# Four residual graph layers in one kernel: a new instruction order between layers 0 and 1 and between layers 2 and 3

## The chip, the cores and the metric

One core of a Trainium2 chip runs the whole kernel in one launch. The metric is the device time of the launch in microseconds (us). Kernels are compared by the median of several runs. The profile is one execution, and its own time stands beside the median below.

## What is computed

Input `x` is 16 batches of 512 nodes x 128 features (f32), `adj` a sparse 512 x 512 matrix. Four layers follow each other, each as `x = layernorm(x + layer(x))`:

```python
# layer 0: eight Euler steps of a graph diffusion
h = einsum('bnd,ed->bne', x, fc_in_w) + fc_in_b
repeat 8: h = h + dt * (alph * 0.5 * (adj @ h - h) + h @ w_eff - h + x0)
# layer 1: normalized graph convolution with two batch norms (statistics over all batches)
agg = einsum('nm,bmd->bnd', A_hat, x);  h = relu(batchnorm(agg @ W1.T + b1));  out = batchnorm(h @ W2.T + b2)
# layer 2: masked attention, 4 heads of 32
scores = q @ k.T / sqrt(32) + mask(adj);  out = softmax(scores) @ v
# layer 3: graph attention with leaky relu scores
e = leaky(s1[:, None] + s2[None, :]) masked by adj;  out = softmax(e) @ (x @ W)
```

## The kernel before

Every engine (PE = TensorE, ACT = ScalarE, DVE = VectorE, POOL = GpSimd, SP = the DMA issuer) has one program of its own, executed in order. Engines meet only in semaphores: `wait_ge` holds an engine's queue until another engine has counted far enough. The order of each engine's work is written out by hand as strings of short item names, and the text below calls an item by its name and batch, as E4.15 for the exponential number 4 of batch 15.

**Layer 0** (`layer0`, from L186) works in 8 groups of two batches. The steps run in a software pipeline `pairs(engine, groups, 5, step)`: step s works on group s (items y, g), on group s-1 (z, p, n, a) and on group s-2 (N, A). `ORDER` (L310) is the order in the middle of the loop, `LAST` (L327) that of step 8, `LATE` (L332) that of step 9. On DVE, p takes a product out of PSUM into `zf` (L684), z forms the low half of a split number (L675), n and N are the layer norm's statistics for the two halves of a group (`statistics` L137 with L141, `aggregate` L143 with L147), and a and A apply the norm and write `X` (`apply`, L182). Between them POOL forms the inverse root (`root`, L149, lines L154 and L156). PE's item p (L893, in `three_pass`, L59 to L61) waits for the low halves z, and its accumulations for the p that freed its bank. `pairs` unrolls the first steps, runs a hardware loop over the middle and unrolls the last ones.

**Layer 1's first half** begins inside steps 8 and 9 of layer 0, since the last products of layer 0 leave gaps. For each batch b: ACT copies the batch to a rounded high part (`batch_high`, L423, line L427); POOL subtracts it for the low part (`batch_low`, L554, line L556, two buffers); PE aggregates (`aggregate`, item a on L963); ACT takes the high part out (L432) and DVE the low part (`aggregate_low`, L648, line L650); PE multiplies by W1 (`hidden`, L973), which waits for that low part; ACT takes it out into `Hb` (L438); DVE adds bn_stats over `Hb` (L817), whose results nobody needs before the end of the layer. PE runs a(b+1) ahead of hidden(b). On POOL, step 9 runs batch_low 2 and 3, then both roots of group 7, and behind the loop come batch_low 4 and 5, two memsets (L595), then batch_low 6. On DVE, step 9 is `#a2 N A`; behind the loop, `aggregate_step` (L809) runs bn_stats for batches 0 and 1, then aggregate_low 3, and so on.

**Layers 2 and 3** (`layers2_3`, L1513) run a loop over 16 batches with about eight steps in flight, and then a hand-written `tail` in which the last batches of layer 2 are mixed with the first of layer 3 (items that begin with 3). Of layer 2, per batch: t0 to t3 on PE are the transposed scores of one head each (L1930, L1934), E0 to E7 on ACT their exponentials, two per head (L1753); S0 to S3 on POOL add the two halves of each head's probabilities (L1678, needs E1, E3, E5, E7 in turn, and the denominators D of the batch before); D0, D1 on PE are the denominators (L1942, wait for all four S); V0 to V3 on PE are the values (L1952, wait for all eight E); e on ACT takes the denominators out (L1763), f the values (L1767); d, o on PE turn both (L1963, L1958); c1, c2 on DVE divide (L1828, L1835; c2 waits for y of the batch before); r on POOL adds the residual (L1684, waits for c2); b on DVE and g2 on POOL are the norm's statistics and root; y on ACT applies it (L175). Of layer 3: 3x turns a batch on PE (L1450), 3XR and 3X on ACT take it out, 3j and 3i on PE form the score rows (L1469, L1476), 3q on PE builds the masked scores (L1499, L1500), 3e on DVE sums, 3E on ACT is the exponential (L1341), 3a on PE the product (L1488).

The tails end, for the last batches:

```python
# POOL
tail("g2.13 S0.15 S1.15 S2.15 r.14 S3.15 g2.14", ...)
# ACT
"... 3W0.0 E2.15 E3.15 f.14 3W1.0 E4.15 E5.15 e.14 E6.15 E7.15 3G.0 3L0.0 3L1.0 y.13 3XR.1 ..."
# PE
"... V2.14 V3.14 3w1.0 t2.15 D0.14 D1.14 3i.0 t3.15 d.14 o.14 V0.15 V1.15 3x.1 V2.15 V3.15 3j.1 D0.15 D1.15 3q0.0 ..."
```

Of the kernel before, what the change touches and what calls it, by code (L numbers as in the profile page):

```python
# [24 lines left out]
ACT = mybir.ActivationFunctionType  # L25
# [56 lines left out]

def pairs(eng, steps, depth, step, first=0, last=None):


    def alive(s):
        return [0 <= s - k < steps for k in range(depth)]

    lead = (depth - 1) + (depth - 1) % 2
    lead = max(lead, first - first % 2)  # L90
    for s in range(first, lead):
        step(s, s % 2, alive(s), s // 2)
    with eng.Fori(lead // 2, steps // 2) as r:
        for parity in range(2):
            step(r * 2 + parity, parity, [True] * depth, r)
    for s in range(steps, steps + depth - 1 if last is None else last + 1):
        step(s, s % 2, alive(s), s // 2)
# [88 lines left out]
def layer0(nc, m, ins, bank, L1):  # L186
# [3 lines left out]
    with ExitStack() as own:  # L190
# [109 lines left out]

        STAGE = dict(h=0, y=0, g=0, z=1, p=1, n=1, a=1, N=2, A=2)

        def order(text):
            items = []
            for word in text.split():
                what, k = (word[:2], int(word[2:])) if word[0] in "#" else (word, sum(w == word for w, _ in items))
                items.append((what, k))
            return items
# [20 lines left out]
            "ACT": order("#x0 #x1 z z z z #a0 z z z z #a1 #h0 #x2 #x3"),  # L329
            "DVE": order("N z z z z A p p #a0 p #w0 p z z z z p p p p #a1 n #W0 #v0 a"),  # L330
        }
        LATE = {"PE": ORDER, "ACT": ORDER, "DVE": order("#a2 N A")}  # L332

        def order_of(s, engine):
            if not isinstance(s, int):
                return ORDER
            return {0: FIRST[engine], 1: SECOND[engine], 2: THIRD[engine], groups: LAST[engine], groups + 1: LATE[engine]}.get(s, ORDER)

# [195 lines left out]
        def _(pool):  # L534
# [30 lines left out]
            def step(s, par, alive, nth):  # L565
# [13 lines left out]
                if alive[2]:  # L579
                    for u in range(2):  # L580
                        norm.root(pool, (s - 2 + CREDIT) * 2 + u, u)
                if isinstance(s, int) and s == 1:
# [4 lines left out]
            pairs(pool, groups, 5, step)  # L587
            for b in range(4, 6):
                batch_low(b, b - 4)
            pool.wait_ge(la_x_lo, after(5, 1))  # L590
# [16 lines left out]
        def _(dve):  # L607
# [46 lines left out]
            def step(s, par, alive, nth):  # L654
                for what, k in order_of(s, "DVE"):
# [21 lines left out]
                    elif what == "p":  # L677
# [8 lines left out]
                    elif what in "nN":  # L686
                        u = "nN".index(what)
                        b = s - STAGE[what]
# [117 lines left out]

            pairs(dve, groups, 5, step)

            def aggregate_step(s, par, alive, nth):  # L809
                early = isinstance(s, int) and s < 4  # L810
                if alive[1] and not early:
                    aggregate_low(s - 1, 1 - par)
                if alive[2]:
                    b = s - 2
                    for c in range(CH):
                        dve.wait_ge(la_h_sb, after(b, CH, c + 1))
                        dve.bn_stats(L1.st1[:, c, bass.ds(b, 1)].rearrange("p a n -> p (a n)"),  # L817
                                     Hb[:, bass.ds(b, 1), c].rearrange("p a n -> p (a n)")).then_inc(la_h_st, 1)

            pairs(dve, B, 5, aggregate_step)  # L820

# [319 lines left out]
def layer3(nc, own, m, bank, out, rl1_at, ready):  # L1141
# [296 lines left out]
    def pe_items(pe):  # L1438

        def item(name, b, par, nth):  # L1440
            what, k = name[0], int(name[1]) if name[-1].isdigit() else 0
            if what == "x":
# [3 lines left out]
                if is_batch(b, 1):  # L1446
                    pe.wait_ge(*ready["second wide"])
                pe.wait_ge(wh_c, after(b - 1, 2))
# [64 lines left out]
def layers2_3(nc, m, bank, wide, out, L1):  # L1513
# [4 lines left out]
    with ExitStack() as own:  # L1518
# [3 lines left out]
        def sem(name):  # L1522
# [16 lines left out]
                 for h in range(2)] + late,  # L1539
# [29 lines left out]
                       {"O": (bn, after(B - 1, 1)), "X": norm.s_x, "score banks": (s_mx, after(B - 1, TILES)),  # L1569
                        "second wide": (t_exp, after(B - 1, EXPS)),  # L1570
                        "ring": ((rcp, after(B - 1, 1)), (o_n, after(B - 1, 1)))})
# [78 lines left out]
        def _(pool):  # L1650
# [39 lines left out]
            third.pool_copy(pool, 1, 1, first=True)  # L1690
            tail("g2.13 S0.15 S1.15 S2.15 r.14 S3.15 g2.14", POOL_ORDER, work, None)
            third.pool_copy(pool, 2, 0, first=True)
# [6 lines left out]
        def _(act):  # L1699
# [13 lines left out]
            def work(name, b, bp, s, alive):  # L1713
# [50 lines left out]
                elif name == "f":  # L1764
# [6 lines left out]
            tail("E0.14 E1.14 E2.14 E3.14 f.13 vc.15 E4.14 E5.14 e.13 nr.15 E6.14 E7.14 3XR.0 3X.0 y.12 E0.15 E1.15 3W0.0 "  # L1771
                 "E2.15 E3.15 f.14 3W1.0 E4.15 E5.15 e.14 E6.15 E7.15 3G.0 3L0.0 3L1.0 y.13 3XR.1 3L2.0 3L3.0 3X.1 f.15 e.15 "
                 "3E0.0 3W0.1 3W1.1 y.14 3E1.0 3XR.2 3G.1 3L0.1 3L1.1 3X.2 3L2.1 y.15", ACT_ORDER, work, item)
# [77 lines left out]
        def _(pe):  # L1851
# [25 lines left out]
            def product(name, b, bp, s, alive):  # L1877
# [82 lines left out]
                elif name == "d":  # L1960
# [7 lines left out]
            pe.wait_ge(third.const, 3)  # L1968
            tail("v.15 t2.14 D0.13 D1.13 n.15 t3.14 3x.0 d.13 o.13 t0.15 3j.0 V0.14 V1.14 t1.15 3w0.0 V2.14 V3.14 3w1.0 t2.15 "
                 "D0.14 D1.14 3i.0 t3.15 d.14 o.14 V0.15 V1.15 3x.1 V2.15 V3.15 3j.1 D0.15 D1.15 3q0.0 3q1.0 d.15 3w0.1 3q2.0 "  # L1970
                 "3w1.1 3q3.0 o.15 3i.1 3x.2 3a0.0 3j.2 3a1.0 3q0.1 3q1.1 3a2.0", PE_ORDER, work, item)
# [38 lines left out]
```

## Time and profile before

| what | us |
|---|---|
| median of 3 runs | 944.48 (944.11 to 945.14) |
| the profiled execution, its own time | 941.33 |
| its span, first to last instruction | 939.5 |
| PE busy | 865.5 (92%) |
| DVE busy | 625.7 (67%) |
| ACT busy | 506.1 (54%) |
| POOL busy | 404.5 (43%) |
| mean granted clock of TensorE | 0.987 of full speed |

A row of the timeline gives start, duration, engine, line, operation, output<-input, shape and count; in square brackets stands how long the engine was idle before, and what released it. Rows of the same kind that follow each other are merged (x4), and the duration is then from the first start to the last end. PE's matmuls overlap, so the next one can start before the one before it has ended. A row of the windows gives the stretch, then each engine's busy time with its count of instructions, the granted clock, the share of DMA and its GB/s.

### The profile page before, as it was taken

How to read it: one execution, taken by the hardware profiler on the slowest of the kernel's cores; microseconds unless marked ns; L12 is line 12 of the kernel's file. 1: busy time of each engine (PE TensorE's matmuls, PEld its weight loads, DVE VectorE, ACT ScalarE, POOL GpSimd, SP SyncE). 2: the span in 40 equal slices, each digit the busy share in tenths (PEclk: the TensorE clock that was granted, in tenths of full speed). 3: DMA queues.
4: the chain of work that ended last, by engine and by line, in shares of the span. 5: the costliest groups of instructions: out<-in, count | busy, mean ns of one | idle time of the engine just before them, and what ended most of it. 6: DMA issues, size and time to landing. Idle time of an engine off the chain costs nothing. (4 is left out here: it accounts for less than half of the span.)

```text
span 939.5 us, 20538 instructions
## 1 busy us (share of the span) xinstructions
PE 865.5 (92%) x6039; PEld 619.4 (66%) x6039; DVE 625.7 (67%) x1931; ACT 506.1 (54%) x903; POOL 404.5 (43%) x451
## 2 busy tenths in 40 slices
PE   6999999999999998978768999999999997899996
PEld 5798999999999887843334444444444443677775
DVE  4756645545545556557686887778876642899997
ACT  4333221211211234666457787878877665888884
POOL 4010210211211225200344788887887776366554
PEclk9999999999999999999979999999999999999998
DMA  9000000000010000000133344333433430010111
GB/s 253 33 12 12 13 12 23 13 13 14 20 34 0 12 1 0 0 0 0 35 69 69 86 99 87 67 77 81 100 79 69 88 83 1 13 34 22 33 33 46
DMA packets 34249, 40.82 MB, mean 43 GB/s; under 512 B 6673, under 2 KB 17553, under 8 KB 34193
## 3 DMA queue, kind: packets, MB, share of 16 engines
q1 hardware_dynamic: 32816, 39.87, 17.8%
q8 instruction: 28, 0.46, 0.2%
q10 hardware_dynamic: 1376, 0.27, 0.1%
q14 instruction: 29, 0.23, 0.1%
HBM read 6.43 MB, written 4.19 MB: 11 GB/s over the span
## 5 line engine op out<-in xcount | busy, mean ns | idle before, releaser
L1678 POOL TENSOR_TENSOR half_sum<-prob 128x1024 f32<-128x1024 f32 x64 | 151.4, 2378 | 21.6 <-PE bank L1942 20.3
L1753 ACT ACTIVATE prob<-wide 128x1024 f32<-128x1024 f32 x128 | 124.2, 1023 | 38.3 <-PE wide L1934 38.1
L458 ACT CAST yT<-wide 128x512 fp32r<-128x512 f32 x48 | 28.1, 588 | 190.9 <-PE wide L862 141.9
L1822 DVE CUSTOM_DVE_ANT_0 junk<-wide,mask_ij 128x512 bf16<-128x512 f32 x128 | 82.7, 684 | 52.1 <-PE bank L1914 51.0
L1930 PE MATMUL wide<-qk_st 128*128 128x512 f32 x256 | 84.5, 435 | 3.2 <-ACT prob L1753 1.7
L1822 DVE CUSTOM_DVE_ANT_0 junk<-bank,mask_ij 128x512 bf16<-128x512 f32 x128 | 83.0, 685 | 0.0
L551 POOL TENSOR_TENSOR Xr<-Xf,Xr 128x512 fp32r<-128x512 f32 x16 | 20.4, 1291 | 140.1 <-ACT Xr L453 139.9
L1488 PEld LDWEIGHTS bank<-Wh,pr 128*128 128x128 f32 x512 | 65.2, 191 | 15.6 <-ACT pr L1341 7.0
L1488 PE MATMUL bank<-Wh,pr 128*128 128x129 f32 x512 | 68.5, 278 | 6.4 <-ACT pr L1341 5.5
L59 PE MATMUL bank<-z,L3T_hi 128*128 128x256 f32 x256 | 72.6, 284 | 1.3 <-DVE z L675 1.3
L61 PE MATMUL bank<-z,L3T_lo 128*128 128x256 f32 x256 | 72.3, 283 | 0.0
L60 PE MATMUL bank<-z,L3T_hi 128*128 128x256 f32 x256 | 72.3, 282 | 0.0
L1930 PEld LDWEIGHTS wide<-qk_st 128*128 128x128 f32 x256 | 46.4, 192 | 30.2 <-DVE mx L1822 19.2
L154 POOL TENSOR_SCALAR n_rstd<-n_aggr 128x4 f32<-128x4 f32 x31 | 7.2, 233 | 135.7 <-DVE n_aggr L147 130.3
L1952 PE MATMUL bank<-prob,v 128*32 128x512 f32 x512 | 61.6, 598 | 1.2 <-ACT prob L1753 1.2
L661 DVE TENSOR_TENSOR yT<-wide,yT 128x512 fp32r<-128x512 f32 x48 | 32.9, 686 | 31.8 <-ACT yT L458 31.8
L59 PEld LDWEIGHTS bank<-z,L3T_hi 128*128 128x128 f32 x256 | 48.7, 190 | 3.4 <-DVE z L675 2.6
L684 DVE TENSOR_TENSOR zf<-bank,G 128x256 f32<-128x256 f32 x64 | 27.0, 421 | 33.7 <-PE bank L61 32.0
L1914 PEld LDWEIGHTS wide<-qkT 32*128 32x128 f32 x128 | 12.3, 184 | 56.2 <-ACT prob L1753 29.6
L60 PEld LDWEIGHTS bank<-z,L3T_hi 128*128 128x128 f32 x256 | 48.8, 191 | 0.4
L61 PEld LDWEIGHTS bank<-z,L3T_lo 128*128 128x128 f32 x256 | 48.9, 191 | 0.0
L1377 DVE SCALAR_TENSOR_TENSOR pr<-bank,Wh,rl 128x512 f32<-128x512 f32 x64 | 44.9, 741 | 5.9 <-PE bank L1500 5.4
(302 smaller groups left out, 2370.9 us busy)
## 6 DMA issues: line engine op xcount, KB each, us to landing
qk_st<-qkT SPq DMA_DIRECT2D x192, 128.0 KB, 2.4
out_dram<-rc SPq DMA_DIRECT2D x15, 256.0 KB, 2.3
Xf<-X SPq DMA_DIRECT2D x14, 256.0 KB, 2.3
A<-in_adj_dram SPq DMA_DIRECT2D x4, 256.0 KB, 4.4
qk_st<-neg_row SPq DMA_DIRECT2D x64, 2.0 KB
Xf<-in_x_dram SPq DMA_DIRECT2D x2, 256.0 KB, 6.8
mask_q<-mask_ji SPq DMA_DIRECT2D x16, 32.0 KB, 1.8
w<-in_L_gnn_W_dram SPq DMA_DIRECT2D x2, 128.0 KB, 2.1
```

What stands on the lines that cost most here:

```text
L59: pe.matmul(out, stat[0], mov[0], start=start, stop=False)
L60: pe.matmul(out, stat[0], mov[1], start=False, stop=False)
L61: return pe.matmul(out, stat[1], mov[0], start=False, stop=stop)
L458: act.copy(yT[bb][i][0][:], psum_y[i][:]).then_inc(y_hi, 1)
L661: dve.tensor_tensor(yT[bb][i][1][:], psum_y[i][:], yT[bb][i][0][:].bitcast(F32), ALU.subtract).then_inc(y_lo, 1)
L1377: dve.scalar_tensor_tensor(out=pr[par][:, k], in0=bank[4 + k % 2][:], scalar=Wh[par][:, k, S2_SLOPE:S2_SLOPE + 1], in1=rl[par][:, k], op0= ...
L1488: last = pe.matmul(out_bank[h][:, t * (D + 2):t * (D + 2) + D + 1], pr[par][:, j, k * P:k * P + P], Wh[par][:, j, 0:D + 1], start=(j == 0) ...
L1678: pool.tensor_tensor(flat(half_sum[h][:]), flat(prob[bp][h][:, 0:2]), flat(prob[bp][h][:, 2:4]), ALU.add).then_inc(h_sum, 1)
L1753: act.activation(flat(prob[bp][h][:, 2 * half:2 * half + 2]), wide[half][:], ACT.Exp, scale=SCALE).then_inc(t_exp, 1)
L1822: dve.tensor_tensor_reduce(out=junk[h % 2][:], in0=ROWS[h][:], in1=m.mask_ij[:, i], scale=1.0, scalar=3.0 * MASKED, op0=ALU.add, op1=ALU.m ...
L1930: pe.matmul(bank[j][:], k_st[:, k, j * P:j * P + P], q_st[:, k], start=True, stop=True)
L1952: last = pe.matmul(ring["V0"][c, :], v[bp][:, k, c], prob[bp][h][:, k], start=(k == 0), stop=(k == NT - 1), skip_group_check=True)
```

## The change

Nothing is added to or taken from what is computed; only orders and one wait differ. At the end of layer 0, the statistics of the second half of group 6 move from the front of DVE's step 8 (N) to the end of step 7 (M). In step 9, DVE runs aggregate_low 3 between N and A; behind it, aggregate_low 4 to 8 each come ahead of the bn_stats of the batches that were waiting, in a list written out. POOL runs batch_low 4 between the two roots of group 7. For this, DVE's loop stops two steps earlier and those steps are unrolled. Between layers 2 and 3, POOL runs S3.15 ahead of r.14; ACT runs e.14 and y.13 ahead of E4.15; PE runs D0.14 and D1.14 ahead of t2.15, and 3x.1 ahead of V0.15 with a wait for seven instead of eight exponentials of batch 15.

```diff
-def pairs(eng, steps, depth, step, first=0, last=None):
+def pairs(eng, steps, depth, step, first=0, last=None, loop_to=None):
...
+    loop_to = steps if loop_to is None else loop_to
+    with eng.Fori(lead // 2, loop_to // 2) as r:
...
+    for s in range(loop_to, steps + depth - 1 if last is None else last + 1):
         step(s, s % 2, alive(s), s // 2)
...
-            "DVE": order("N z z z z A p p #a0 p #w0 p z z z z p p p p #a1 n #W0 #v0 a"),
+            "DVE": order("z z z z A p p #a0 p #w0 p z z z z p p p p #a1 n #W0 #v0 a"),
         }
-        LATE = {"PE": ORDER, "ACT": ORDER, "DVE": order("#a2 N A")}
+        LATE = {"PE": ORDER, "ACT": ORDER, "DVE": order("#a2 N #a3 A")}
+        WHOLE = {"PE": ORDER, "ACT": ORDER, "DVE": order("h h y z z N y z z y A p p g p g g p g y z z y z z y p p g g n p p M g g a")}
...
                     for u in range(2):
+                        if u == 1 and isinstance(s, int) and s == groups + 1:
+                            batch_low(4, 0)
                         norm.root(pool, (s - 2 + CREDIT) * 2 + u, u)
...
-            for b in range(4, 6):
-                batch_low(b, b - 4)
+            batch_low(5, 1)
...
-            pairs(dve, groups, 5, step)
+            pairs(dve, groups, 5, step, loop_to=groups - 2)
...
+            for b, behind in ((4, (0,)), (5, (1, 2)), (6, (3, 4)), (7, (5, 6)), (8, (7,))):
+                aggregate_low(b, b % 2)
+                for k in behind:
+                    hidden_statistics(k)
+            pairs(dve, B, 3, aggregate_step, first=10)
...
                 if is_batch(b, 1):
-                    pe.wait_ge(*ready["second wide"])
+                    pe.wait_ge(*ready["first two"])
...
-            tail("g2.13 S0.15 S1.15 S2.15 r.14 S3.15 g2.14", POOL_ORDER, work, None)
+            tail("g2.13 S0.15 S1.15 S2.15 S3.15 r.14 g2.14", POOL_ORDER, work, None)
...
-                 "E2.15 E3.15 f.14 3W1.0 E4.15 E5.15 e.14 E6.15 E7.15 3G.0 3L0.0 3L1.0 y.13 3XR.1 3L2.0 3L3.0 3X.1 f.15 e.15 "
+                 "E2.15 E3.15 f.14 3W1.0 e.14 y.13 E4.15 E5.15 E6.15 E7.15 3G.0 3L0.0 3L1.0 3XR.1 3L2.0 3L3.0 3X.1 f.15 e.15 "
...
-            tail("v.15 t2.14 D0.13 D1.13 n.15 t3.14 3x.0 d.13 o.13 t0.15 3j.0 V0.14 V1.14 t1.15 3w0.0 V2.14 V3.14 3w1.0 t2.15 "
-                 "D0.14 D1.14 3i.0 t3.15 d.14 o.14 V0.15 V1.15 3x.1 V2.15 V3.15 3j.1 D0.15 D1.15 3q0.0 3q1.0 d.15 3w0.1 3q2.0 "
+            tail("v.15 t2.14 D0.13 D1.13 n.15 t3.14 3x.0 d.13 o.13 t0.15 3j.0 V0.14 V1.14 t1.15 3w0.0 V2.14 V3.14 3w1.0 D0.14 D1.14 "
+                 "t2.15 3i.0 t3.15 d.14 o.14 3x.1 V0.15 V1.15 V2.15 V3.15 3j.1 D0.15 D1.15 3q0.0 3q1.0 d.15 3w0.1 3q2.0 "
```

## Rows read from the trace of the kernel before

**Rows 1.** Windows, all engines: layer 0, the start of layer 2, before D0.15.

```profile
75.00:325.00 250.00, 249.61 (x1572) 235.33 (x1571) 136.02 (x389) 51.54 (x117) 35.78 (x41) 1.00 0.05 16
453.00:460.00 7.00, 3.64 (x19) 2.18 (x19) 3.06 (x17) 5.18 (x11) 3.75 (x8) 1.00 0.00 0
788.00:792.00 4.00, 0.36 (x5) 0.21 (x8) 1.25 (x8) 1.67 (x4) 3.76 (x3) 0.91 0.00 0
```

**Rows 2.** Timeline of PE, around its three stalls between layers 0 and 1.

```profile
325.49 0.39 PE L61 MATMUL wide<-AhT_hi,Xa 128*128 128x512 f32 x1
326.85 0.39 PE L59 MATMUL bank<-z,L3T_hi 128*128 128x256 f32 x1 [0.96 <-DVE z L675]
...
351.14 0.40 PE L61 MATMUL wide<-agT,W1T 128*128 128x512 f32 x1
353.04 0.50 PE L59 MATMUL wide<-AhT_hi,Xa 128*128 128x512 f32 x1 [1.50 <-POOL Xa L556]
...
355.70 0.39 PE L61 MATMUL wide<-AhT_hi,Xa 128*128 128x512 f32 x1
357.94 0.49 PE L59 MATMUL bank<-agT,W1T 128*128 128x512 f32 x1 [1.84 <-DVE agT L650]
```

**Rows 3.** Timeline of DVE, the work ahead of those stalls.

```profile
324.08 0.86 DVE L141 BATCH_NORM_STATS2 n_stats<-zf 128x6 f32<-128x128 f32 x4
...
325.39 1.40 DVE L675 TENSOR_TENSOR z<-G,z 128x256 fp32r<-128x256 f32 x4
...
351.90 2.92 DVE L182 TENSOR_SCALAR X<-zf,n_aggr,n_rstd 128x128 f32<-128x128 f32 x4 [1.66 <-POOL n_rstd L156]
354.74 2.46 DVE L817 BATCH_NORM_STATS2 st<-Hb 128x6 f32<-128x512 f32 x4
357.12 0.67 DVE L650 TENSOR_TENSOR agT<-wide,agT 128x512 fp32r<-128x512 f32 x1
```

**Rows 4.** Timeline of ACT: copy of batch 4, high part of aggregate 3, copy of batch 5.

```profile
348.36 0.61 ACT L427 CAST Xa<-X 128x512 fp32r x1
350.26 0.58 ACT L432 CAST agT<-wide 128x512 fp32r<-128x512 f32 x1 [1.30 <-PE wide L61]
...
352.25 0.61 ACT L427 CAST Xa<-X 128x512 fp32r x1
```

**Rows 5.** Timeline of POOL: batch_low 4 and 5, then two memsets.

```profile
351.71 2.51 POOL L556 TENSOR_TENSOR Xa<-X,Xa 128x512 fp32r<-128x512 f32 x2
...
355.13 3.66 POOL L595 MEMSET qk_st<- 32x2048 f32 x2
```

**Rows 6.** Timeline of PE in the tail: t2.15, D.14, V.15 begins, D.15.

```profile
775.45 1.17 PE L1930 MATMUL wide<-qk_st 128*128 128x512 f32 x4
...
776.91 1.92 PE L1942 MATMUL bank<-half_sum,ones_hd 128*32 128x512 f32 x16
...
783.38 1.92 PE L1952 MATMUL bank<-prob,v 128*32 128x512 f32 x16 [1.17 <-ACT prob L1753]
...
791.82 3.33 PE L1942 MATMUL bank<-half_sum,ones_hd 128*32 128x512 f32 x16 [3.64 <-POOL half_sum L1678]
```

**Rows 7.** Timeline of ACT in the tail: e.14, E6.15 with E7.15, y.13.

```profile
778.92 0.59 ACT L1763 COPY denT<-bank 128x512 f32<-128x512 f32 x1
781.30 1.94 ACT L1753 ACTIVATE prob<-wide 128x1024 f32<-128x1024 f32 x2 [1.79 <-PE wide L1934]
...
785.43 1.65 ACT L175 ACTIVATE X<-rb,n_shift,n_rstd 128x128 f32<-128x128 f32 x4
```

**Rows 8.** Timeline of DVE in the tail: c2.14.

```profile
787.21 0.69 DVE L1835 TENSOR_TENSOR rb<-bank,rec 128x512 f32<-128x512 f32 x1 [5.14 <-ACT X L175]
```

**Rows 9.** Timeline of POOL in the tail: S0.15 to S2.15, r.14, S3.15.

```profile
779.02 7.01 POOL L1678 TENSOR_TENSOR half_sum<-prob 128x1024 f32<-128x1024 f32 x3 [2.98 <-PE bank L1942]
788.10 1.27 POOL L1684 TENSOR_TENSOR rb<-rb,X 128x512 f32<-128x512 f32 x1 [2.07 <-DVE rb L1835]
789.33 2.34 POOL L1678 TENSOR_TENSOR half_sum<-prob 128x1024 f32<-128x1024 f32 x1
```

More of the change, by code:

```diff
@@ L92, in pairs @@
         step(s, s % 2, alive(s), s // 2)
-    with eng.Fori(lead // 2, steps // 2) as r:
+    loop_to = steps if loop_to is None else loop_to
+    with eng.Fori(lead // 2, loop_to // 2) as r:
         for parity in range(2):
             step(r * 2 + parity, parity, [True] * depth, r)
-    for s in range(steps, steps + depth - 1 if last is None else last + 1):
+    for s in range(loop_to, steps + depth - 1 if last is None else last + 1):
         step(s, s % 2, alive(s), s // 2)
@@ L299, in layer0 @@
         block = own.enter_context(nc.Block())
-        STAGE = dict(h=0, y=0, g=0, z=1, p=1, n=1, a=1, N=2, A=2)
+        STAGE = dict(h=0, y=0, g=0, z=1, p=1, n=1, a=1, M=1, N=2, A=2)
         def order(text):
@@ L336, in order_of @@
                 return ORDER
-            return {0: FIRST[engine], 1: SECOND[engine], 2: THIRD[engine], groups: LAST[engine], groups + 1: LATE[engine]}.get(s, ORDER)
+            return {0: FIRST[engine], 1: SECOND[engine], 2: THIRD[engine], groups - 1: WHOLE[engine], groups: LAST[engine], groups + 1: LATE[engine]}.get(s, ORDER)
         def four(u):
@@ L685, in step @@
                                           G[1 - par][:, 1 if k < NT else 0, t], ALU.add).then_inc(h_sb, 1)
-                    elif what in "nN":
-                        u = "nN".index(what)
+                    elif what in "nNM":
+                        u = int(what != "n")
                         b = s - STAGE[what]
@@ L805, in step, with hidden_statistics @@
                                                  op1=ALU.subtract).then_inc(v_Ah, 1)
-            pairs(dve, groups, 5, step)
+            pairs(dve, groups, 5, step, loop_to=groups - 2)
+            def hidden_statistics(b):
+                for c in range(CH):
+                    dve.wait_ge(la_h_sb, after(b, CH, c + 1))
+                    dve.bn_stats(L1.st1[:, c, bass.ds(b, 1)].rearrange("p a n -> p (a n)"),
+                                 Hb[:, bass.ds(b, 1), c].rearrange("p a n -> p (a n)")).then_inc(la_h_st, 1)
             def aggregate_step(s, par, alive, nth):
-                early = isinstance(s, int) and s < 4
-                if alive[1] and not early:
+                if alive[1]:
                     aggregate_low(s - 1, 1 - par)
                 if alive[2]:
[L814 to L820, printed above, removed]
+                    hidden_statistics(s - 2)
+            for b, behind in ((4, (0,)), (5, (1, 2)), (6, (3, 4)), (7, (5, 6)), (8, (7,))):
[3 more added lines that the diff above has]
+            pairs(dve, B, 3, aggregate_step, first=10)
         @block.tensor
@@ L1569, in layers2_3 @@
                        {"O": (bn, after(B - 1, 1)), "X": norm.s_x, "score banks": (s_mx, after(B - 1, TILES)),
-                        "second wide": (t_exp, after(B - 1, EXPS)),
+                        "second wide": (t_exp, after(B - 1, EXPS)), "first two": (t_exp, after(B - 1, EXPS, EXPS - 1)),
                         "ring": ((rcp, after(B - 1, 1)), (o_n, after(B - 1, 1)))})
```

## The prediction

> **What bounds the kernel now.** I read the windows first, then PE's timeline at the two places that the change touches, then the timelines of the engines that PE waits for there. The windows [rows 1] show layer 0 as a stage that PE alone sets: 249.61 us busy in 250. Every other engine has room there, so an order on DVE counts in layer 0 only where PE runs out of work. That happens three times, all at the end of layer 0 [rows 2]: 0.96 us for the low halves z, 1.50 us for batch_low 4 of POOL, 1.84 us for aggregate_low 3 of DVE, 4.30 us in all. The second place is the tail between layers 2 and 3. There PE stands idle for 3.64 us in front of D0.15 and then takes 3.33 us for 16 matmuls [rows 6] that took 1.92 us for batch 14 [rows 6], because the granted clock had gone from full speed (2.4 GHz) toward half (1.2 GHz): the mean over 788 to 792 us is 0.91, with PE busy for 0.36 of 4 us [rows 1].
>
> **Boundary of layers 0 and 1, first stall.** PE's first p of step 8 needs four z. DVE runs them at 325.39 for 1.40 us, right behind the statistics N, which began at 324.08 [rows 3]. The change takes N (1.31 us, from 324.08 to 325.39) from there, so the z run from 324.1 to 325.5. PE's last matmul of #a0 starts at 325.49, and the pitch of that kind is 0.23 us, so p can start at 325.72 instead of 326.85: **1.13 us**. N is not gone: as M it sits in step 7 between the last p and the last two g. There it costs DVE the same 1.31 us, beside a PE that never starves; the next g is held up by some 0.1 us, and PE needs the bank behind it only a whole product later. I cost it at nothing; if that cover were gone it would cost at most 1.31 us. Its root on POOL then comes before A asks for it, so A no longer holds DVE.
>
> **Second stall.** PE waits for batch_low 4, because POOL runs it behind the second root of group 7: the two batch_low 4 and 5 start at 351.71 and take 2.51 us, 1.26 us each [rows 5]. ACT had the batch ready at 348.97 [rows 4]. In the new order POOL takes it between the roots. With everything 1.13 us earlier (first stall gone), ACT is through at 347.85 and POOL at 349.2. PE asks for it 0.23 us behind the matmul of 351.14 [rows 2], thus at 350.24 on the new clock, and it is there 1 us early. Gain 353.04 - 351.37 = **1.67 us**. Queued behind the inserted batch_low is the second root. Before, A started 1.66 us behind the statistics that ended at 350.24 [rows 3]; they now end at 349.1, POOL is free 0.1 us later, so A starts near 350.85.
>
> **Third stall.** hidden(3) needs aggregate_low 3, at 357.12 on DVE. Ahead of it stood A, for 2.92 us, and four bn_stats, for 2.46 us [rows 3], though ACT had the input ready at 350.84 [rows 4]. In front of A it runs from 349.7 to 350.4. PE asks for it at 355.93 - 1.13 - 1.67 = 353.1, so it is early by more than 2 us. Gain 357.94 - 355.93 = **2.01 us**. What was moved behind are bn_stats, which nobody reads before the layer ends, and each aggregate_low from 4 to 8 stands ahead of them.
>
> **What is late next** is POOL. ACT's copy of batch 5, at 352.25 [rows 4], comes 1.13 us earlier, so batch_low 5 runs from 351.8 to 353.05. batch_low 6 stands behind that and behind two memsets of 3.66 us [rows 5], which also wait for A; they started 0.3 us behind A's end before. So they run from 353.35 to 357.0 and batch_low 6 until 358.3. PE asks for it at 358.6 (two aggregations of 12 matmuls and two hidden of 6, at 0.23 us, behind 350.24). That fits by 0.3 us. Sum of the boundary: 1.13 + 1.67 + 2.01 = **4.8 us**; its low end is the same less what POOL could be late.
>
> There is a contention, too: A's four operations took 2.92 us while POOL ran the two batch_low of 2.51 us [rows 3, 5]. The Trainium skill ("Advanced Engine Details and Errata", VectorE Performance Modes, Mode Summary) says that the second SBUF port of VectorE is shared with GpSimd, so that two-port Vector instructions and GpSimd's block each other; the trace agrees with that 2.92 us. It speaks against POOL's work beside A. I place three of A's four operations ahead of batch_low 5, so the sum keeps 4.8; the other case is a rival.
>
> **Boundary of layers 2 and 3.** The chain before is y.13 on ACT until 787.08 [rows 7], c2.14 on DVE until 787.90 [rows 8], r.14 on POOL, S3.15 until 791.67 [rows 9], D0.15 at 791.82 [rows 6]. The new chain, step by step:
> - PE: D0.14 and D1.14 take the place of t2.15, which started at 775.45 [rows 6]. They end at 777.3 (1.85 us), t2.15 at 778.8 (1.46 us, from 775.45 to 776.91).
> - ACT: e.14 (0.46 us net of 0.59 [rows 7]) at 777.4, as soon as D1.14 is out (the same 0.1 us behind it as before), y.13 (1.55 us net) until 779.45. This holds E4.15 and E5.15 (0.92 us each) until 781.3, then t3.15 (1.46 us) until 782.9, then E6.15, E7.15 until 784.8. Before, they ended at 783.24 [rows 7]. So the exponentials pay **1.6 us** for the early y.13.
> - POOL: S0.15 to S2.15 wait for D1.14 and take 7.01 us [rows 9]: 777.5 to 784.5. S3.15 has its exponential at 784.8, runs until **787.4**, and r.14 follows.
> - PE: V.15 can start at 785.0 instead of 783.38 [rows 6]. 3x.1 now runs in the gap before it, once E6.15 is out at 783.9. So V.15 ends at 785.0 + 2 x 1.86 = 788.7, and 3j.1 (0.45 us) at 789.2, later than S3.15. D.15 starts at 789.2, now behind work and not behind a wait, at full clock: until 791.05.
> - Before, D.15 ended at 795.15. Gain **4.1 us**: 2.6 us of the start and 1.5 us of the clock.
>
> Queued behind the moved items: behind S3.15, r.14 (1.27 us) until 788.7, then b.14 on DVE until 790.0, ahead of 3e0.0 at 791.8; g2.14 and both copies until 793.3, and PE wants the first copy at 795.4. c2.14 is early now, since y.13 is. 3XR.1 and 3X.1 end by 789.3, before 3w0.1. So all that follows D.15 moves as one, and layer 3's loop begins in the same relative state. SP's queue is not touched in either place.
>
> **Sum.** 4.8 + 4.1 = 8.9 us. Against the profiled execution of 941.33 us (span 939.5) it gives 932.4. The median of the runs lies 3.15 us above that execution; the work taken away is the same in both, so I forecast 944.48 - 8.9 = **935.6 us**, on its own 934.6 to 936.8. The low-clock stretches at the start of later stages begin wherever PE falls idle, and a shift by 5 us can lengthen or shorten each; I allow 1 us for it.
>
> **Rivals.**
> 1. *POOL or the shared port takes over the first boundary.* If A falls beside batch_low 5, it waits for that one's 1.26 us, the memsets wait for A, and PE waits for batch_low 6. This is where the rule named above would act. Time 935.6 + 1.3 = 936.9. For it: a margin of 0.3 us, and A that reaches to the start of batch_low 5. Against: the memsets wait for batch_low 5 anyway, so only what A lasts longer counts. Chance 0.13.
> 2. *The clock falls in the thinner tail.* From 779.9 to 785.0 PE now has only t3.15 and 3x.1, some 2.1 us of work in 5.1. If the clock drops there, V.15 and D.15 run wholly or partly at half speed: 1.5 us for D.15 (3.33 - 1.85) and as much for each slow half of V.15. With D.15 and a bit over one half of V.15 slow it is 3.4 us, time 939.0. Against: in 453 to 460 us PE was busy 3.64 of 7 us and the clock stayed at 1.00 [rows 1]; before 791 it took over 3 us without any work. Chance 0.08.
> 3. *The named waits were not the only ones.* Another producer stands right behind at the first boundary and only its first stall goes: 4.1 + 1.1 = 5.2 us, time 939.3. Chance 0.04. The stronger form, that the change doesn't do what it says because both stalls come back one step later (PE waiting for DVE's delayed bn_stats at layer 1's end, or for E7.15): 943 to 945, chance 0.04.
> 4. *Slower than before: layer 3's loop locks into another phase.* Its 13 turns pass work around PE, ACT, DVE and POOL. If y.14 and the copies arrive in another relative order and each turn becomes p longer, it costs 13 p. It decides from p = 0.68 us; with p = 1 us the time is 944.48 - 8.9 + 13 = 948.6. For it: no engine is full there for long, so the turns hang on the order of arrival. Against: everything behind D.15 shifts by the same 4.1 us. Chance 0.03.
>
> **How the numbers follow.** Forecast 0.68, rivals 0.13, 0.08, 0.04 + 0.04, 0.03. A run of this kernel tells about 0.2% (1.9 us) from no change. Faster by more: 0.68 + 0.13 + 0.08 + 0.04 = 0.93; within: 0.04; slower: 0.03. The range goes from 934.0 (the sum plus the allowance for the clock) to 939.5, which holds rivals 1 and 2.
>
> **What would show it.** PE's idle rows of 0.96, 1.50 and 1.84 us gone, and layer 1's last product 4.8 us earlier. If rival 1 holds, a stall of PE for `Xa` of L556 stands three products later. In the tail, S3.15 ahead of r.14, D.15 of 1.9 us instead of 3.33, behind 3j.1 and without idle time; E7.15 ending 1.6 us later than before, less the 4.8 of before. If D.15 is again over 3 us, or V.15 over 1.92, rival 2 holds. The prediction is wrong if the unrolled steps 6 and 7 let PE starve in layer 0, which no row of before can show.

## The result, and the profile after

The changed kernel takes 933.53 us (median of 4 runs, 932.98 to 933.80) where the kernel before, run beside it, takes 944.30: a ratio of 0.9887, 95% interval 0.9870 to 0.9904. The forecast was 935.6, its range 934.0 to 939.5. So the direction was right, and the time fell 0.5 us out of the range at the low end. The profiled execution took 933.39 us, with a span of 931.6.

PE's timeline at the boundary of layers 0 and 1 in the kernel after (columns as in [rows 2]): the last matmul of #a0 and the first p, then the two places where it had waited in [rows 2].

```profile
325.69 0.40 PE L61 MATMUL wide<-AhT_hi,Xa 128*128 128x512 f32 x1
325.92 0.28 PE L59 MATMUL bank<-z,L3T_hi 128*128 128x256 f32 x1
...
349.99 0.40 PE L61 MATMUL wide<-agT,W1T 128*128 128x512 f32 x1
350.22 0.40 PE L59 MATMUL wide<-AhT_hi,Xa 128*128 128x512 f32 x1
...
352.79 0.40 PE L61 MATMUL wide<-AhT_hi,Xa 128*128 128x512 f32 x1
353.02 0.40 PE L59 MATMUL bank<-agT,W1T 128*128 128x512 f32 x1
```

All three stalls are gone: each matmul starts 0.23 us behind the one ahead of it. Their producers, DVE first (N's place is empty, A and aggregate_low 3 have changed places against [rows 3]), then POOL (against [rows 5]):

```profile
324.28 1.42 DVE L678 TENSOR_TENSOR z<-G,z 128x256 fp32r<-128x256 f32 x4
...
349.74 0.69 DVE L653 TENSOR_TENSOR agT<-wide,agT 128x512 fp32r<-128x512 f32 x1 [0.63 <-ACT agT L434]
350.77 1.12 DVE L183 TENSOR_SCALAR X<-zf,n_aggr,n_rstd 128x128 f32<-128x128 f32 x4 [0.34 <-POOL n_rstd L157]
```

```profile
347.89 1.29 POOL L558 TENSOR_TENSOR Xa<-X,Xa 128x512 fp32r<-128x512 f32 x1 [1.97 <-ACT Xa L429]
...
351.79 1.30 POOL L558 TENSOR_TENSOR Xa<-X,Xa 128x512 fp32r<-128x512 f32 x1 [1.18 <-ACT Xa L429]
...
353.32 3.66 POOL L598 MEMSET qk_st<- 32x2048 f32 x2
357.07 1.29 POOL L558 TENSOR_TENSOR Xa<-X,Xa 128x512 fp32r<-128x512 f32 x1
```

The tail before layer 3 on PE, the lines that answer to [rows 6]: D.14 now ahead of t2.15, t3.15, V.15, 3j.1, D.15.

```profile
769.62 1.92 PE L1950 MATMUL bank<-half_sum,ones_hd 128*32 128x512 f32 x16
771.47 1.20 PE L1938 MATMUL wide<-qk_st 128*128 128x512 f32 x4
...
775.70 1.93 PE L1938 MATMUL wide<-qk_st 128*128 128x512 f32 x4 [1.61 <-ACT prob L1761]
...
780.41 3.64 PE L1960 MATMUL bank<-prob,v 128*32 128x512 f32 x32 [0.23 <-ACT prob L1761]
783.98 0.50 PE L1477 MATMUL wide<-xTr,wB 128*128 128x512 f32 x1
784.41 1.92 PE L1950 MATMUL bank<-half_sum,ones_hd 128*32 128x512 f32 x16
```

D.15 starts without a wait and takes 1.92 us, as D.14 does. What is new is t3.15: it waits 1.61 us for the exponentials E5.15, which e.14 and y.13 hold up, and takes 1.93 us instead of the 1.20 of t2.15. ACT and POOL there, against [rows 7, 9]:

```profile
771.61 0.59 ACT L1771 COPY denT<-bank 128x512 f32<-128x512 f32 x1 [1.35 <-PE bank L1950]
772.09 1.65 ACT L176 ACTIVATE X<-rb,n_shift,n_rstd 128x128 f32<-128x128 f32 x4
773.64 1.91 ACT L1761 ACTIVATE prob<-wide 128x1024 f32<-128x1024 f32 x2
778.33 1.94 ACT L1761 ACTIVATE prob<-wide 128x1024 f32<-128x1024 f32 x2 [2.77 <-PE wide L1942]
```

```profile
771.73 7.00 POOL L1686 TENSOR_TENSOR half_sum<-prob 128x1024 f32<-128x1024 f32 x3 [1.49 <-PE bank L1950]
780.34 2.39 POOL L1686 TENSOR_TENSOR half_sum<-prob 128x1024 f32<-128x1024 f32 x1 [1.62 <-ACT prob L1761]
782.70 1.28 POOL L1692 TENSOR_TENSOR rb<-rb,X 128x512 f32<-128x512 f32 x1
```

Where the 7.9 us between the two spans (939.5 and 931.6) went, from the starts above and those of [rows 2, 6]:

| stretch | before | after | gain | forecast |
|---|---|---|---|---|
| start to the last matmul of #a0 | 325.49 | 325.69 | -0.2 | 0 |
| from there to hidden(3) | 32.45 | 27.33 | 5.1 | 4.8 |
| to t2.15, in after D.14 | 417.51 | 416.60 | 0.9 | 0 |
| to the end of D.15 | 19.70 | 16.71 | 3.0 | 4.1 |
| layer 3, to the end | 144.35 | 145.27 | -0.9 | 0 |

### The profile page after: what moved, and what is told of

It is laid out like the page before. It is cut to its first block and busy times, and to the rows that moved or that the text cites. A ratio compares the mean times of both kernels' runs of the same rounds, so it can differ in the third digit from the quotient of the medians.

```text
span 931.6 us, 20358 instructions
## 1 busy us (share of the span) xinstructions
PE 864.7 (93%) x6039; PEld 619.7 (67%) x6039; DVE 624.1 (67%) x1931; ACT 506.6 (54%) x903; POOL 404.0 (43%) x451
## 5 line engine op out<-in xcount | busy, mean ns | idle before, releaser
L558 POOL TENSOR_TENSOR Xa<-X,Xa 128x512 fp32r<-128x512 f32 x16 | 20.6, 1293 | 59.8 <-ACT Xa L429 59.8
```

## The experiments

Each time stands beside executions of the kernel before on the same chip: their medians were 943.39 in the first comparison (the first four runs), 942.91 in the second (the next four), 943.35 in the third, 942.82 in the fourth. The variants are named as in the texts on record.

| run | median, us (lowest to highest) | ratio, 95% |
|---|---|---|
| before_again | 943.44 (941.23 to 947.02) | 0.9981 to 1.0025 |
| after_again | 933.27 (932.27 to 934.06) | 0.9848 to 0.9908 |
| first_only | 938.00 (936.62 to 939.16) | 0.9902 to 0.9956 |
| second_only | 938.71 (936.48 to 939.82) | 0.9914 to 0.9959 |
| warm_tail | 941.16 (939.06 to 946.69) | 0.9959 to 0.9997 |
| warm_both | 940.46 (938.51 to 945.92) | 0.9957 to 0.9998 |
| pool_swap | 937.94 (935.71 to 943.87) | 0.9927 to 0.9973 |
| best | 932.87 (931.77 to 934.65) | 0.9862 to 0.9918 |
| pad_12 | 932.89 (931.92 to 933.17) | 0.9859 to 0.9897 |
| pad_64 | 934.13 (932.14 to 938.09) | 0.9870 to 0.9907 |
| first_pool | 933.16 (931.25 to 939.18) | 0.9871 to 0.9925 |
| unroll_only | 944.79 (944.36 to 946.17) | 1.0005 to 1.0029 |
| fill_best | 933.11 (931.02 to 935.08) | 0.9855 to 0.9916 |
| fill_before | 942.80 (940.42 to 948.24) | 0.9977 to 1.0022 |
| fill_pad | 932.42 (930.73 to 933.29) | 0.9848 to 0.9907 |
| low4_late | 935.41 (935.04 to 936.48) | 0.9884 to 0.9943 |

**Both kernels again.**

> The kernel before, unchanged, timed against itself. The medians moved by 10.8 us, the two profiled spans only by 7.9 us (939.5 to 931.6). Theory A (the kernel before has a place whose length varies between executions, and the execution shown was a quick one): the runs spread over 2 to 3 us, most spans lie near 942, and a profile of such an execution is longer than 939.5 us in one place, behind the idle time before D0.15 or in the loop of layer 3. Theory B (a passing difference between chips or hours): all spans near 939.5, ratio to itself 1.000 and the spread under 1 us.

> The changed kernel, unchanged. Theory A: 933.0 to 934.0 again with a spread under 1 us, ratio near 0.9885. Theory B: the ratio is nearer to 0.9915 (8 us less than before).

The gain of the medians is 10.1 us here, where the first runs gave 10.8. Theory A is right about the spread, which is larger than it says: the single executions of before_again lie up to 5.8 us apart, those of after_again 1.8. It is wrong about the place. The profiled execution of before_again comes to t2.15 0.65 us later than that of before (776.10 and 775.45), and its tail is no longer (19.50 and 19.70 us, from the start of t2.15 to the end of D.15).

**Each half of the change alone.** first_only keeps all edits of layer 0 and 1 and puts the three orders of the tail back; second_only is the kernel before with this:

```diff
-tail("g2.13 S0.15 S1.15 S2.15 r.14 S3.15 g2.14", POOL_ORDER, work, None)
+tail("g2.13 S0.15 S1.15 S2.15 S3.15 r.14 g2.14", POOL_ORDER, work, None)
...
-     "E2.15 E3.15 f.14 3W1.0 E4.15 E5.15 e.14 E6.15 E7.15 3G.0 3L0.0 3L1.0 y.13 3XR.1
+     "E2.15 E3.15 f.14 3W1.0 e.14 y.13 E4.15 E5.15 E6.15 E7.15 3G.0 3L0.0 3L1.0 3XR.1
...
-     3w1.0 t2.15 D0.14 D1.14 3i.0 t3.15 d.14 o.14 V0.15 V1.15 3x.1 V2.15 V3.15 3j.1
+     3w1.0 D0.14 D1.14 t2.15 3i.0 t3.15 d.14 o.14 3x.1 V0.15 V1.15 V2.15 V3.15 3j.1
```

> Only the new order between layers 0 and 1; the tail between layers 2 and 3 as before. If the two places add up: 4.9 to 5.2 us less than before, ratio 0.9946. If the first place also shifts something in layer 2's loop (the two traces drift apart by another 0.6 us there): 5.5 to 5.8 us less. Theory A with its varying place in the tail: this kernel's runs spread as those of before; with the place elsewhere they don't.

> Only the new order between layers 2 and 3. The traces give 3.0 us at the end of D.15 (8.8 less 5.8) and 1.0 us given back in layer 3: 2.0 to 3.0 us less, ratio 0.997 to 0.998. Theory A with its varying place in the tail: 5 to 6 us less in the median, ratio 0.994, and the spread of before is gone. The prediction had 4.1 us for this part.

The halves give 5.4 and 4.7 us, together 10.1, which is what both give together. They don't get in each other's way. The second half, with 4.7, lies between what the traces had given for it (2.0 to 3.0) and theory A (5 to 6).

**The clock of the two stalls alone.** warm_tail fills PE's idle time ahead of D0.15 in the kernel before with matmuls into a bank that nobody reads, and takes no wait away; warm_both does so at two stalls of the first boundary as well. For that it also writes out six steps of PE's loop in layer 1, which changes the length of PE's program ahead of layer 3.

```diff
+                    if k == 0 and isinstance(b, int) and b == B - 1:
+                        for _ in range(14):
+                            pe.matmul(bank[3][:], m.identb[:], m.mask_ji[:, 0], start=True, stop=True)
                     if k == 0:
                         pe.wait_ge(h_sum, after(b, H))
```

> The kernel before, with 14 extra matmuls (bf16, 128x512, 0.22 us each, 3.0 us in all) into a free bank between 3j.1 and D0.15, where PE stands idle for 3.64 us. They change no order and no result. Theory A1 (the kernel before loses 2 to 3 us in the median to low-clock stretches that its idle times bring on, and most of it in the tail): D.15 takes 1.9 us instead of 3.33, median 1.5 to 3 us less than before, spread smaller. Theory A2 (the low-clock stretches that differ from execution to execution lie elsewhere, at the boundary of layers 0 and 1 or at the start of layer 2): D.15 is quick, the median falls by 1.5 us at most and the spread stays at 5 us or more.

> As warm_tail, and also 6 extra matmuls ahead of aggregation 4 (1.3 us of a gap of 1.67) and 8 ahead of hidden 3 (1.7 us of a gap of 2.0). Theory A2, with the boundary of layers 0 and 1 as the place: no low-clock stretch near 359 us, median another 1 to 1.5 us below warm_tail. Theory A1: the same time as warm_tail within 0.5 us. If extra matmuls delayed the real ones, it would be slower by 0.3 us at most.

PE's timeline of warm_tail: the fillers, then D.15.

```profile
789.43 2.97 PE L1941 MATMUL wide<-mask_ji,identb 128*128 128x512 bf16 x13
792.92 1.92 PE L1945 MATMUL bank<-half_sum,ones_hd 128*32 128x512 f32 x16 [0.52 <-POOL half_sum L1678]
```

D.15 takes 1.92 us instead of 3.33 with the same wait for POOL: the 1.5 us that the forecast put down to the clock are shown, and the median falls by 1.75 us. The smaller spread of theory A1 did not come: the executions still reach from 939.06 to 946.69. In the medians, the fillers at the first boundary bring nothing that can be told (940.46 and 941.16, with intervals that overlap), but warm_both doesn't settle it. Its profiled execution comes to t2.15 1.84 us before that of warm_tail (774.79 and 776.63) and loses 2.0 us again near the end of layer 3, where DVE waits 3.2 us instead of 1.2 for one store of the output. Whether that wait is in every execution, and whether the written-out steps bring it, no run here shows.

**What in the tail does it.** pool_swap is the kernel before with the first line of the diff above alone. best is the kernel after with t2.15 ahead of D.14 again, and on ACT `E4.15 E5.15 e.14 y.13 E6.15 E7.15`. first_pool is first_only with POOL's line.

> The kernel before with one edit: POOL runs S3.15 ahead of r.14. PE and ACT keep their orders. The exponentials then end as before (783.24) and S0.15 to S2.15 at 786.03, so S3.15 ends at 788.4 and D.15 starts at 788.5 instead of 791.82, 3.3 us earlier, and with a short idle time the clock stays: 1.4 us more. Theory C (PE's and ACT's new orders in the change cost more than they bring, since the swap alone takes away the wait): median as low as that of second_only or up to 1.5 us lower (937 to 938.7). Rival: y.13, still late on ACT, or c2.14 behind it takes the place of the wait removed, and it is slower than second_only (over 939.5).

> The changed kernel, but in the tail PE runs t2.15 ahead of D0.14 again, and ACT runs E4.15, E5.15, e.14, y.13, E6.15, E7.15: y.13 in the gap in which ACT waits for t3.15. 3x.1 ahead of V0.15, S3.15 ahead of r.14 and the whole first boundary stay as in the change. Theory C: the exponentials end 1.6 to 2.4 us earlier than in the change, PE has no idle time before t3.15 and no low clock in t3.15, D.15 starts 1.7 us earlier: 931.5 us against 933.3. Rival: D.15 isn't what the tail hangs on, since 3e0.0 waits for b.14, and it gains under 0.5 us.

> The whole change at the boundary of layers 0 and 1, and of the change before layer 3 only the swap on POOL (S3.15 ahead of r.14); PE and ACT keep the order of before. The first part alone gave 938.0 and the swap alone 937.9, 5.4 and 5.0 us under before. Theory A2 (the swap is the whole gain of the tail, the rest is about even): 932.6 to 933.3, equal to after within 0.5 us. Rival (the gains overlap, because a part of each is the low-clock stretches that either may avoid): 934 to 935.5. Layer 3's turns 17.19.

PE in pool_swap, t2.15 and D.15, and the same two in best:

```profile
777.57 1.15 PE L1930 MATMUL wide<-qk_st 128*128 128x512 f32 x4
...
790.61 1.92 PE L1942 MATMUL bank<-half_sum,ones_hd 128*32 128x512 f32 x16 [0.34 <-POOL half_sum L1678]
```

```profile
769.77 1.15 PE L1938 MATMUL wide<-qk_st 128*128 128x512 f32 x4
...
782.82 1.92 PE L1950 MATMUL bank<-half_sum,ones_hd 128*32 128x512 f32 x16 [1.08 <-POOL half_sum L1686]
```

From the start of the first to the end of the last it is 14.96 us in pool_swap and 14.97 in best, 16.71 in after and 19.70 in before; first_pool has 14.97 as well. So POOL's S3.15 ahead of r.14 carries the whole gain of the tail, 4.7 us, and the new orders of PE and ACT cost some of it: in second_only and after_again, whose t3.15 runs at full clock (1.16 us), the stretch from D.14 is 15.7 us. This 0.8 us is seen in the rows; the whole runs (933.27 in after_again, 933.16 in first_pool, 932.87 in best) can't be told apart.

**One stall of the first boundary.** low4_late is the kernel after with batch_low 4 behind the second root again:

```diff
-                        if u == 1 and isinstance(s, int) and s == groups + 1:
-                            batch_low(4, 0)
                         norm.root(pool, (s - 2 + CREDIT) * 2 + u, u)
...
-            batch_low(5, 1)
+            for b in range(4, 6):
+                batch_low(b, b - 4)
```

> The kernel after with one thing put back: batch_low 4 stands on POOL behind both roots of group 7 again, ahead of batch_low 5. This undoes the second stall's cure alone. In after, POOL began batch_low 4 at 347.89 and PE asked for it at about 350.2; DVE's statistics end near 349.6, the second root is done near 350.0, batch_low 4 then from 350.0 to 351.3. Theory A: PE waits about 1.1 us for it before aggregate 4 (out of the 1.50 of before, since everything is earlier there), batch_low 5, the memsets and batch_low 6 all fall 1.3 us later and aggregate 6 waits too, so 1.1 to 1.6 us in all: 934.4 to 935.1. Rival: what stands there is hidden (another wait was the later one): 933.3, as after.

PE, DVE and POOL in low4_late:

```profile
351.77 0.50 PE L59 MATMUL wide<-AhT_hi,Xa 128*128 128x512 f32 x1 [1.50 <-POOL Xa L558]
```

```profile
350.64 2.92 DVE L183 TENSOR_SCALAR X<-zf,n_aggr,n_rstd 128x128 f32<-128x128 f32 x4 [0.34 <-POOL n_rstd L157]
```

```profile
350.45 2.52 POOL L558 TENSOR_TENSOR Xa<-X,Xa 128x512 fp32r<-128x512 f32 x2
```

The stall is back with its 1.50 us, and the time is 2.1 us over that of after_again, while before itself was 0.6 us lower in this comparison: the second term (1.67) is shown, and the whole run costs 2.1 to 2.7. My expectation of 1.1 us for the wait was low, and 935.41 lies just above the 934.4 to 935.1. The later wait for batch_low 6 that I had expected did not come: the 1.50 us are PE's only listed wait from 320 to 362 us. A takes 2.92 us again, beside POOL, where it took 1.12 in after with POOL idle. By the Trainium skill ("Advanced Engine Details and Errata", VectorE Performance Modes, Mode Summary) two-port work of VectorE and GpSimd block each other on a shared port; this pair of rows agrees, and shows that the order on POOL decides whether they meet.

**Writing the steps out.** unroll_only is the kernel before with this and nothing moved:

```diff
-            pairs(dve, groups, 5, step)
+            pairs(dve, groups, 5, step, loop_to=groups - 2)
```

> The kernel before, with steps 6 and 7 of DVE's loop in layer 0 written out instead of looped, in the same order; nothing is moved, so all three stalls of PE stay and the tail is unchanged. Its layer 3 then stands 30 instructions earlier in DVE's program than before. Theory A (the order at the boundary is the gain): 943 to 943.5, the same as before, three stalls of 0.96, 1.50 and 1.84 us. Rival (writing the steps out is what helps layer 0): one or more of the stalls is shorter and the time 0.5 to 2 us less. For the spread: single executions of before reach 945 to 949; if those hang on DVE's program, they are gone here, if on the stalls, they stay. Theory P: layer 3's turns differ from 17.04.

PE's longest waits from 320 to 362 us in unroll_only (us in total, times, longest):

```profile
PE bank L59 <- DVE agT L651: 1.8, 1, 1.8
PE wide L59 <- POOL Xa L557: 1.5, 1, 1.5
PE bank L59 <- DVE z L676: 1.0, 1, 1.0
```

The three stalls stay: the new order removes them, not the written-out steps. By itself the edit costs 1.4 us, against the expected 943 to 943.5, with a mean granted clock of 0.978 to 0.982 in all 12 executions. The profiled one comes to t2.15 at 778.68 us, 3.2 us later than that of before, with a granted clock of 0.77 instead of 0.88 over 456 to 500 us. Why this edit lowers the clock there, and why the change, which contains it, doesn't show that loss, stays open.

**Layer 3's 0.9 us.** The order of layer 3 is untouched, yet its turns are longer. pad_12 and pad_64 add, on best, instructions that do nothing in DVE's idle time before c1.14 (two waits make one instruction):

```diff
                 elif name == "c1":
+                    for _ in range(24 if isinstance(b, int) and b == 14 else 0):
+                        dve.wait_ge(rcp, 1)
```

> The kernel 'best' with 24 waits (two to an instruction, so 12 instructions) on a semaphore that has long arrived, put on DVE in its idle time of 5.24 us before c1.14. Nothing else changes. DVE's program of layer 3 then stands at the same place as in the kernel before, 12 instructions further on than in after and best. In all six profiles with DVE's old program two turns of layer 3's loop take 8.72 + 8.32 = 17.04 us; in all four with the new one 8.74 + 8.45 = 17.19 us. Theory P (the place of DVE's loop in its program costs it): the turns go back to 17.04, and the time falls by six times 0.15, 0.9 us: 932.0 where best has 932.9. Rival Q (the phase in which work arrives at the loop): the turns stay at 17.19 and the time within 0.3 us of best.

> As the run with 12 instructions, but with 128 waits, 64 instructions, in the same gap, which is long enough for them at up to 0.08 us each. Theory P: the turns take some value other than 17.19, since the loop lies elsewhere again; 17.04 or something third. Rival Q: 17.19 as in best, or a change only if the waits overrun the gap, which would show as c1.14 later than 776.1.

DVE's waits from 812 to 912 us in best, pad_12 and pad_64:

```profile
DVE junk L1377 <- issue: 4.0, 12, 0.5
```

```profile
DVE junk L1377 <- issue: 2.8, 6, 0.5
```

```profile
DVE junk L1377 <- issue: 3.7, 6, 0.6
```

SP's stores of the output in best and pad_12, five in a row (from the first issue to the end of the last):

```profile
825.32 34.76 SPq L1243 DMA_DIRECT2D out_dram<-rc  x5
```

```profile
826.75 34.52 SPq L1243 DMA_DIRECT2D out_dram<-rc  x5
```

Four turns take 0.24 us less in pad_12, 0.12 for each two, and the "issue" waits of DVE ahead of 3m fall from 12 to 6 ("issue" is idle time for which the profile shows no other engine as the cause). Over all fifteen stores the same is seen: 118.90 us in best, 117.89 in pad_12 and 118.08 in before. fill_best and fill_pad, the same pair with fillers in layer 2, repeat it (118.88 and 117.83). The waits overran DVE's gap a little: against the start of D.15, c1.14 comes 0.2 us later in pad_12 than in best, and 0.9 in pad_64. But rival Q, the phase, is out by the halves of the change: second_only has the tail of after and 118.03 us, first_only the tail of before and 118.86. The turns go with DVE's program, whatever the tail does, and where the loop stands in that program is what pad_12 moves. So theory P holds for the turns.

The recorded texts are wrong about where it stands. Counted in the programs that the kernels build into, the change puts 88 instructions more ahead of layer 3's loop (70 of them by the written-out steps), and pad_12 puts it 12 further still, not back to the place of before:

| kernel | DVE instructions ahead of layer 3's loop | two turns, us | "issue" waits in 100 us |
|---|---|---|---|
| before | 1584 | 17.04 | 2.8 us, 6 |
| unroll_only | 1654 | 17.07 | 2.8 us, 6 |
| after, best | 1672 | 17.19 | 4.0 us, 12 |
| pad_12 | 1684 | 17.07 | 2.8 us, 6 |
| pad_64 | 1736 | 17.21 | 3.7 us, 6 |

So a longer program is not a slower one, and no run here says which place is good. unroll_only keeps nearly the turn of before, against my expectation. Nor does pad_12 give all of the 0.9 us back: from the end of D.15 to the end of the span, before has 144.35 us, best 145.26 and pad_12 144.82, since pad_12 takes 3.3 us behind the end of its last store and best 2.7 (fill_pad and fill_best: 144.78 and 145.25). The medians of pad_12 (932.89) and best (932.87) are the same; the effect is seen in the turns alone.

The Trainium skill ("Runtime: NRT & Kernel Launch", Instruction fetch mechanics) says that a taken branch to outside the fetched window stalls for a fetch. The rows have the waits once in each two turns or once in each, which would fit a branch, but the trace doesn't bear it out: from 870 to 925 us best has five of these waits on DVE (1.5 us) and its DMA queues not one instruction packet. What the "issue" waits are stays open.

**What the medians have beyond the profiles.** fill_best, fill_before and fill_pad add ten fillers to PE at the start of layer 2, on best, before and pad_12:

```diff
-... ("s0", 3): 4, ("s1", 3): 3, ("s2", 3): 3}
+... ("s0", 3): 4, ("s1", 3): 3, ("s2", 3): 3, ("q", 3): 5, ("k", 4): 3, ("x", 4): 2}
```

> The kernel 'best' with ten more bf16 filler matmuls of 0.24 us on PE (their output goes to a bank that nobody reads then), in the idle time of the start of layer 2: five behind q of step 3, three behind k and two behind x of step 4, so 2.4 us of work into waits of 1.8, 0.9 and 0.6 us between 464 and 472 us. The granted clock is 0.88 over 456 to 500 us in best and in every quick profile, 0.77 in unroll_only (944.49) and 0.69 in pad_64 (938.09). Theory S (the spread and part of the time are the low clock of that stretch, which follows the thin work of PE before it): the mean of 456 to 500 goes to 1.00 or near it, the time falls by 1 to 3 us to 930 to 932, and no execution is above 935. Rival T (the clock does not follow this work, or DVE and ACT set the pace there anyway): the mean or the time stay, 932.5 to 933.5.

> The same ten fillers in the kernel before. Theory S: the spread of the single executions of before (941.2 to 947.5 in the last comparison, median 943.35, with the mean clock from 0.974 to 0.987) shrinks, none is above 944, and the median falls to 939.5 to 941.5, since the quick executions of before lose the low clock of 456 to 500 too. Rival T: median 943 to 943.5 and the spread as before.

> The fillers and the 12 instructions on DVE together, on the kernel best. In the run with the 12 instructions alone, layer 3's turns went back to 8.75 + 8.33 us. If both effects are what they were taken for, layer 3 starts as in the run with the fillers alone and its turns are 17.08 in place of 17.19: 0.3 to 0.7 us under that run.

Windows of pad_64 and of fill_best (columns as in [rows 1]; the third figure from the end is the granted clock), and the first V of layer 2 in each:

```profile
464.00:478.00 14.00, 11.40 (x42) 6.57 (x42) 11.00 (x37) 3.72 (x7) 3.19 (x6) 0.51 0.05 10
478.00:492.00 14.00, 11.33 (x67) 6.94 (x64) 9.73 (x34) 6.58 (x10) 7.10 (x8) 0.52 0.53 115
...
501.64 1.92 PE L1962 MATMUL bank<-prob,v 128*32 128x512 f32 x16
```

```profile
464.00:478.00 14.00, 11.54 (x55) 5.94 (x56) 12.83 (x42) 3.79 (x7) 3.43 (x6) 0.87 0.13 29
478.00:492.00 14.00, 10.09 (x88) 5.95 (x88) 8.65 (x31) 9.71 (x14) 6.92 (x7) 0.76 0.45 96
...
498.11 1.92 PE L1961 MATMUL bank<-prob,v 128*32 128x512 f32 x16
```

Both executions come to the same matmul at 464.65 us (to 0.01). pad_64 then runs at half clock (0.51 and 0.52 are near 1.2 GHz) through both windows and comes to V 3.53 us later than fill_best: this execution took 938.09 us, the kernel's median is 934.13. fill_best does this although it has the ten fillers to run as well. So a long low stretch at the start of layer 2 accounts for most of this outlier (at t2.15 the two are 4.6 us apart, at the end 4.4). fill_best has 0.87 and 0.76 there, and no execution over 935.1. But the median of fill_best is no lower than that of best, and fill_before keeps its spread, up to 948.24: the fillers don't hold the clock up in general. The theory on record, that this stretch is the spread, is half right: one place of it is shown, not all, and not what sets it. Theory S's 930 to 932 us and 939.5 to 941.5 us did not come. fill_pad, at 932.42 the lowest median of all, has the turn of pad_12 again; that it beats best is not shown.

## Why the prediction was wrong by its number, and which of its mechanisms held

**The step that failed** is the base: "the work taken away is the same in both, so I forecast 944.48 - 8.9". I took the 3.15 us between the median and the profiled execution of before to stay. They didn't. The kernel after has a median 0.14 us above its own profiled execution (933.53 and 933.39). Sorted by mean granted clock, 96 executions of before and before_again are: 12 up to 0.979, with a median of 947.8 us; 47 from 0.980 to 0.984, at 943.7; 28 at 0.985 and 0.986, at 942.3; 9 at 0.987, at 941.1. Of the 10 of after and after_again none is under 0.985, and the 8 from 0.987 up have 933.3. So at about the same clock the change brings 7.8 us, as the two profiles say (7.94), and the other 2 to 3 us of the medians go with executions of before that have more time at low clock. The profiled one, with 0.987, was among the quickest tenth, and that was chance. I had allowed 1 us for the clock, and had thought of stretches that shift, not of ones that most executions have and the profiled one lacks. The miss would have been larger without a second error: the base was 3.0 us too high, and the sum of 8.9 was 1.0 too large, which leaves the 2.1 us between 935.6 and 933.53.

What in the change takes the slow executions away is not shown. 37 of 96 executions have 0.985 or more in before, 4 of 7 in first_only, 6 of 9 in second_only, 46 of 51 in the kernels with both, which looks as if each half takes a part of them away. But fill_before has 10 of 12 and a median no lower than before's (942.80 and 942.82), so the count doesn't stand for time, and 7 and 9 executions are few. Why an execution falls into the low stretches stays open too: unroll_only has none of 12 at 0.985 or more with an order of work that is the same as before's.

**First boundary, 4.8 us:** right, 5.1 measured. The first p starts 0.23 us behind #a0, the term of 1.13. Terms two and three are right to the row: 1.90 us between the matmuls around each wait became 0.23 (1.67), 2.24 became 0.23 (2.01). The other 0.3 us lie mostly right behind the waits, where the second matmul follows the first about 0.1 us late: in before the second p starts 0.22 us behind the first, in after 0.12. M cost nothing that can be told: the last matmul of #a0 starts between 325.3 and 325.8 us in the profiles of either order.

**POOL as the next limit:** batch_low 6 was placed at 357.0 to 358.3 and ran from 357.07 to 358.36. Rival 1 did not come: A took 1.12 us, from 350.77 on, and batch_low 5 began at 351.79, beside its last 0.1 us.

**The tail, 4.1 us:** 3.0 measured in the profiled execution, 4.0 in after_again (from D.14 at 771.33 to the end of D.15 at 787.06, against 19.70), so the working was right at full clock and a clock that falls in the thin part took 1.0. Of four profiled executions with this order only that of after has it; second_only, after_again and low4_late have t3.15 at 1.16 us. That is rival 2 in a mild form: the window from 768 to 800 us has 0.95 in after and 1.00 in after_again, and it is t3.15 that pays (1.93 us instead of 1.16), with the transposes behind it, not D.15 or V.15. Its price was put at 3.4 and is 1.0. What I did not see is that it was the sum of a gain of 4.7 from POOL's order and a loss of 0.8 from the rest.

**"All that follows D.15 moves as one":** wrong by 0.9 us. The place of DVE's loop in its program is not the same, and moving it by 12 instructions (pad_12) gives 1.0 us back in the turns, of which 0.6 is lost again behind the last store. Rival 4 had the form (a turn becomes longer) and the wrong mechanism and size: 0.07 us a turn, not 0.68.

**Layers 1 and 2, 0:** they gave 0.9, within the allowance. Two executions of one kernel differ by more there: from the first p to D.14 it is 443.70 us in after and 445.61 in after_again. So the 0.9 needs no edit behind it, and none is shown.

## What to carry over

A single profiled execution fixes the terms of a sum but not the base that they are taken from: compare its granted clock with those of the timed executions first, and where the median lies well above the profile, price the case that the excess goes with the stalls. When a wait hangs on one operation at the end of a queue, try the smallest swap on that queue by itself; the orders on the other engines that look as if they belong to it may cost. An edit that changes the length of one engine's program can change loops that it doesn't touch.

## What was not expected of the hardware

- 12 instructions that do nothing, put ahead of a loop on DVE, shorten its turns by 0.06 us each: "issue" waits of 2.8 us instead of 4.0 in 100. With 52 more the turns are as long as without any (17.21 and 17.19 us for two).
- From the same point, pad_64 came 3.5 us later to the first values product of layer 2 than fill_best, which has ten fillers more to run: the granted clock over 464 to 492 us was 0.51 instead of about 0.8. The execution's mean was 0.976.
- In 96 executions of one program the time follows the mean granted clock with a correlation of -0.94, from a median of 947.8 us up to 0.979 to one of 941.1 at 0.987. The ten executions of the program after are all within 1.8 us.
